# The last spectral mixing of a four-layer convolution kernel, as 32x32 products on the array's diagonal tiles

## What is computed

```
def _L3_conv_ref(x, weights):
    x_f = jnp.fft.rfft2(x)
    k_f = jnp.fft.rfft2(weights)
    out_f = jnp.einsum('bchw,ochw->bohw', x_f, k_f)
    return jnp.fft.irfft2(out_f, s=(H, W))
```

## Time and profile before

| What | us |
|---|---|
| median of 3 runs | 1059.65 |
| lowest, highest | 1059.22, 1061.24 |
| the profiled execution's own time | 1059.79 |
| its span in the trace | 1058.0 |
| PE busy | 894.0 |
| DVE busy | 661.6 |
| ACT busy | 520.3 |

### The profile page before, as it was taken

How to read it: one execution, slowest core, us unless ns; L and a number is a source line. 1 busy time by engine, 2 the same in 40 slices (tenths; PEclk the granted TensorE clock), 3 DMA queues, 4 the chain that set the end, 5 groups by cost and what they waited for, 6 DMA issues and landing times. The chain is left out here.

```text
span 1058.0 us, 25662 instructions
## 1 busy us (share of the span) xinstructions
PE 894.0 (85%) x9335; PEld 742.2 (70%) x9335; DVE 661.6 (63%) x1208; ACT 520.3 (49%) x900; POOL 122.2 (12%) x120
## 2 busy tenths in 40 slices
PE   6999999776468956488699999995888799998998
PEld 6999999765367953376544444443887699998998
DVE  3556464674585769689776665655666698871232
ACT  2444444575434437166379996001887423325554
POOL 0000000001001006156302222000000100001110
PEclk9999999898658989699899999997999899999999
DMA  6465757463300000000000000002200337740222
GB/s 251 160 241 192 271 212 220 119 155 81 93 4 1 0 14 1 0 1 0 0 1 1 0 0 0 0 0 52 44 0 0 80 81 159 145 94 1 95 105 117
DMA packets 47673, 79.12 MB, mean 75 GB/s; under 512 B 19322, under 2 KB 37888, under 8 KB 44816
## 3 DMA queue, kind: packets, MB, share of 16 engines
q1 hardware_dynamic: 30992, 61.80, 21.1%
q10 hardware_dynamic: 16640, 16.78, 4.6%
HBM read 50.65 MB, written 27.92 MB: 74 GB/s over the span
## 5 line engine op out<-in xcount | busy, mean ns | idle before, releaser
L1440 DVE SCALAR_TENSOR_TENSOR X<-bank,c_power,X 32x512 f32 x128 | 95.8, 748 | 60.4 <-PE bank L1408 55.4
L1565 PE MATMUL bank<-m_xp,m_kf 128*32 128x64 f32 x2048 | 116.8, 224 | 6.5 <-DVE m_xp L1533 5.1
L1565 PEld LDWEIGHTS bank<-m_xp,m_kf 128*32 128x32 f32 x2048 | 116.4, 139 | 6.9 <-issue 6.9
L1408 PE MATMUL bank<-c_rh,c_w_high 128*128 x288 | 111.0, 386 | 2.0 <-DVE c_rl L1353 2.0
L1408 PE MATMUL bank<-c_rh,c_w_low 128*128 x288 | 110.9, 385 | 0.0
L1408 PE MATMUL bank<-c_rl,c_w_high 128*128 x288 | 110.8, 385 | 0.0
L924 DVE TENSOR_TENSOR X<-X,bank 128x512 f32 x64 | 43.6, 681 | 91.2 <-PE bank L910 91.2
L205 DVE BATCH_NORM_STATS2 bn<-X 128x6 f32 x128 | 85.5, 683 | 2.4 <-POOL X L1212 1.6
L1581 ACT COPY xm<-bank 64x512 f32 x64 | 32.5, 585 | 95.3 <-PE bank L1565 95.3
L1367 ACT ACTIVATE c_r<-X,c_nrm 32x1024 f32 (+1 forms) x56 | 73.4, 1311 | 2.4 <-DVE c_nrm L1416 1.1
L439 DVE COPY ks_cols<-bank 128x512 f32<-128x512 f32 x64 | 42.6, 681 | 46.0 <-PE bank L405 46.0
(11 more groups left out here) (187 smaller groups left out, 1931.2 us busy)
## 6 DMA issues: line engine op xcount, KB each, us to landing
ks_src<-in_L_conv_weights SPq DMA_DIRECT2D x32, 512.0 KB, 6.3
kf<-ks_spec ACTq DMA_DIRECT2D x16, 1024.0 KB, 10.1
m_kf<-kf SPq DMA_DIRECT2D x32, 512.0 KB, 8.0
X<-in_x SPq DMA_DIRECT2D x4, 2048.0 KB, 12.9
out_y<-X SPq DMA_DIRECT2D x16, 512.0 KB, 2.7
xf<-f_xm SPq DMA_DIRECT2D x6, 448.0 KB
l_wb<-in_L_conv_weights_r SPq DMA_DIRECT2D x4, 512.0 KB, 13.0
l_wb<-in_L_conv_weights_i SPq DMA_DIRECT2D x4, 512.0 KB, 14.7
```

The costliest lines, as they stand in the source:

```text
L1408: m = pe.matmul(ps[n][:], w[:, ky, kx].rearrange("p o c -> p (o c)"), d[:, q, b, y:y + HALF, x:x + HN], start=i == 0, stop=i == len(terms) ...
L1440: dve.scalar_tensor_tensor(x, ps[n][o * C:(o + 1) * C, :].rearrange("p (y x) -> p y x", x=HN), filt.power[at, 2:3], x, ALU.mult, ALU.add). ...
L1565: last = pe.matmul(ps[4 * half + m // 8][at:at + C, m % 8 * N:(m % 8 + 1) * N], kf[p][:, j, :, H * half + m], xp[half][:, j, m].rearrange( ...
```

## The change

The last mixing takes xm as it lies. For each set, DVE writes a buffer xt with two parts: the spectra as they are, and the spectra multiplied by i (imaginary part negated, real part behind it). PE multiplies part 0 with the real part of the kernel's spectra and part 1 with the imaginary part, and adds the two in PSUM. Each product has 32x32 weights and 32x32 data, on one quarter g of the partitions, and writes the same quarter of the output; the four quarters follow one another, each at another frequency k so that they write to four different banks. That is 8 x 64 x 2 x 4 = 4096 products; the loop's body holds 1024 of them and is run four times. POOL's zeros are gone. ACT copies a whole set of 128 partitions out of PSUM. The kernel's spectra are loaded by one transfer of 2 MB for each set, in the layout in which kf lies in DRAM. In the first stage the stores of kf move from ACT's stream to SP's.

```diff
@@ kernel_spectra_stage, SP's stream
-                with sp.Fori(0, tiles // 2) as i:
-                    for p in range(2):
-
-                        sp.wait_ge(turned, START + 32 * i + 16 * p - 16)
-                        for k in range(4):
...
+                def store(i, p):
+                    sp.wait_ge(made_read, START + 32 * i + 16 * p + 16)
+                    for part in range(2):
+                        sp.dma_start(pr.kf[:, :, part, 2 * i + p, :].rearrange("s p n -> p s n"),
+                                     spec[:, :, part].rearrange("p s o k -> p s (o k)")).then_inc(stored, 16)
+
+                for p in range(2):
+                    load(0, p)
+                load_x(0)
+                with sp.Fori(1, tiles // 2) as i:
+                    for p in range(2):
+                        load(i, p)
+                        store(i - 1, p)
+                    load_x(i)
+                for p in range(2):
+                    store(tiles // 2 - 1, p)
                 filt.load(sp)
@@ kernel_spectra_stage, ACT's stream
-                        act.wait_ge(made_read, START + base + 16)
-                        for part in range(2):
-                            act.dma_start(pr.kf[:, :, part, 2 * i + p, :].rearrange("s p n -> p s n"),
-                                          spec[:, :, part].rearrange("p s o k -> p s (o k)")).then_inc(stored, 16)
@@ load_kernel_spectra
+    sp.dma_start(to[:].rearrange("p r o k -> p (r o k)"), pr.kf[s].rearrange("p r t n -> p (r t n)")
+                 ).then_inc(loaded, 16)
@@ l3_mix_stage, DVE's stream
+            def turn(dve, s, p):
+
+                dve.tensor_copy(xt[p][:, 0], xm[:, s])
+                dve.tensor_scalar(xt[p][:, 1, :, 0], xm[:, s, :, 1], -1.0, None, ALU.mult)
+                return dve.tensor_copy(xt[p][:, 1, :, 1], xm[:, s, :, 0])
...
@@ l3_mix_stage, PE's stream
+                with pe.Fori(0, SETS // 2) as i:
                     for p in range(2):
...
+                        for t in range(N):
+                            for part in range(2):
+                                for g in range(4):
+
+                                    k = (t + SPAN * g) % N
+                                    at = slice(g * C, (g + 1) * C)
+                                    last = pe.matmul(ps[4 * p + k // SPAN][at, k % SPAN * 2 * B:(k % SPAN + 1) * 2 * B],
+                                                     kf[p][at, part, :, k], xt[p][at, part, k].rearrange("p r b -> p (r b)"),
+                                                     start=part == 0, stop=part == 1)
+                        last.then_inc(mixed, 1)
@@ l3_mix_stage, ACT's stream
+                        act.wait_ge(mixed, START + 2 * i + p + 1)
+                        for n in range(4):
+                            c = act.copy(xm[:, 2 * i + p, SPAN * n:SPAN * n + SPAN].rearrange("p k r b -> p (k r b)"),
+                                         ps[4 * p + n][:])
+                        c.then_inc(mixed_read, 1)
```

More of the change, by code:

```diff
@@ L1455, in _ @@
             def _(sp):
-                load_kernel_spectra(sp, pr, kf0, 0, 0, loaded0)
+                load_kernel_spectra(sp, pr, kf0, 0, loaded0)
             @block.tensor
@@ L1502, in _ @@
             def _(sp):
-                load_kernel_spectra(sp, pr, kf[1], 0, 1, loaded[1])
-                with sp.Fori(1, PAIRS) as i:
+                load_kernel_spectra(sp, pr, kf[1], 1, loaded[1])
+                with sp.Fori(1, SETS // 2) as i:
                     for p in range(2):
[L1507 to L1520, removed]
+                        sp.wait_ge(mixed, START + 2 * i + p - 1)
+                        load_kernel_spectra(sp, pr, kf[p], 2 * i + p, loaded[p])
@@ L1535, in _ @@
[L1535 to L1538, removed]
-                    for p in range(2):
-                        for half in range(2):
-                            dve.wait_ge(mixed, START + 4 * i + 2 * p + half - 1)
-                            stage(dve, i, p, half).then_inc(staged, 2)
-            @block.gpsimd
-            def _(pool):
-                pool.memset(xp[0][0:2 * C, :, :, 1], 0.0).then_inc(zeroed, 1)
-                pool.memset(xp[0][2 * C:P, :, :, 0], 0.0).then_inc(zeroed, 1)
+                for p in range(2):
+                    last = turn(dve, p, p)
+                    if p == 0:
+                        packed = slice(0, N, N // 2)
+                        last.then_inc(fix, 1)
+                        dve.wait_ge(fix, 1)
+                        dve.memset(xt[0][0:C, 0, packed, 1], 0.0)
+                        dve.memset(xt[0][0:C, 1, packed, 0], 0.0)
+                        last = dve.tensor_copy(xt[0][0:C, 1, packed, 1], xm[0:C, 0, packed, 1])
+                    last.then_inc(turned, 1)
@@ L1549, in _ @@
+                with dve.Fori(1, SETS // 2) as i:
+                    for p in range(2):
+                        dve.wait_ge(mixed, START + 2 * i + p - 1)
+                        turn(dve, 2 * i + p, p).then_inc(turned, 1)
             @block.tensor
@@ L1552, in _ @@
                 pr.keep_warm(pe, 16)
[L1553 to L1554 removed]
+                with pe.Fori(0, SETS // 2) as i:
                     for p in range(2):
[L1556 to L1569 removed]
+                        pe.wait_ge(loaded[p], 16 * i + 16)
+                        pe.wait_ge(turned, 2 * i + p + 1)
+                        pe.wait_ge(mixed_read, START + 2 * i + p - 1)
+                        pe.sem_inc(pr.pace, 1)
+                        for t in range(N):
[7 more added lines that the diff above has]
+                        last.then_inc(mixed, 1)
             @block.scalar
@@ L1573, in _ @@
                 act.sem_inc(mixed_read, START)
[L1574 removed]
+                with act.Fori(0, SETS // 2) as i:
                     for p in range(2):
[L1576 to L1583 removed]
+                        act.wait_ge(mixed, START + 2 * i + p + 1)
[3 more added lines that the diff above has]
+                        c.then_inc(mixed_read, 1)
 def matrices(pr, ctx, shapes, dt=F32):
```

59 lines of the change are left out of this document (11 added, 48 removed).

## The result

| | before | after |
|---|---|---|
| median of the device time | 1059.43 us (4 runs) | 1224.71 us (4 runs) |
| ratio after / before | | 1.1548 [1.153, 1.1565] |
| span of the profiled execution | 1058.0 us | 1223.0 us |
| last mixing, first to last start of a record on PE | 118.5 us | 273.2 us |
| first product of the input transform (L237) | 200.97 us | 212.12 us |

A forecast was written before the change was run, and what follows sets the result against it. PE was taken as the bound, with fetching of code setting the new mixing's time: +130 mixing, -3 earlier start, +0.3 last copies, +15 first stage, +142 on 1059.8, 1202 us; 8-in-10 range 1125 to 1255.

The forecast's parts named there:

- The blocks: Last mixing on PE: 4 passes of 16 blocks of 256 instructions, each fetched anew in 3.73 us, 239 us.
- one and a half blocks already there: Start of the last mixing: the first code is already fetched, which saves only its stops, about -1 us.
- The jumps: Last mixing's loop: each of three jumps back costs one more block, 11 us together; ends none to 3 x 7.5.
- Queueing behind the loads of kf: Last mixing: a fetch may queue during 2 MB loads, 0 to 1.3 us each third block, up to 29 us.
- The clock does not enter: Last mixing: even at 1.2 GHz a block's 128 records take 2.42 us, less than the 3.73 of fetching.
- The first stage: End of the first stage: small loads now stand behind a store, delaying the next stage +15 us, ends +5 and +22.
- The earlier start: Last mixing: DVE's first staging takes 3.4 us, so PE starts earlier, -3 us.
- hidden staging, copies and loads of 2 MB: Last mixing: DVE's 3 us, ACT's 2.3 us and the loads of a set stay hidden under 31 us of PE.
- Rival 1: Last mixing: the loop body stays after its first pass; stage 118 to 176 us, total 1071 to 1129; chance 0.13.
- Rival 2: Last mixing: blocks fetched ahead, four quarters overlapping at full clock, 9.4 ns a record, 77 us; total 1030; chance 0.06.
- The stops: First layer's mixing: PE stops 1.0 to 1.6 us after each 128 records, read as waiting for the next code block.
- The 25 ns floor: Skill's claim that matmuls start no less than about 25 ns apart: stage 205 us, total about 1158; given no chance.

The follow-up runs named there:

- e2: Changed kernel with the four loop passes of the last mixing written out on PE, so no jump back: 1198.04 us, ratio 1.1319.
- e5: Changed kernel without the six 2 MB loads of kf inside the last mixing: 1203.97 us, ratio 1.1387.
- e1: Changed kernel with PE's mixing loop body cut to 4 blocks, the first 16 t multiplied four times, still 8192 records: 1088.87 us, ratio 1.0284.
- e8: First stage of the changed kernel with the last mixing of the kernel before: 1070.10 us, ratio 1.0113.
- e4: Changed kernel with all t from 32 on left out, so a body of 8 blocks and 4096 records: 1105.45 us.
- e6: e1 with 16 data columns in each product instead of 32: stage 135.4 us.
- e12: e1 with 64 data columns in each product instead of 32: stage 140.1 us.

## Why the prediction was right

**The blocks (239 us of the sum).** Right in kind and size. 67 large distances, 70 packets in the mixing (26 to 92 in all, "60 or more" was asked for), mostly 3.5 to 3.8 us from start to start. The -1 us for one and a half blocks already there did not come: PE stopped for 4.20 us after its first 127 records. e2, which has no jumps, took 248.5 us for 64 blocks; by the prediction 239.

**The jumps (11 us): the term that was mis-sized.** Three times one more block of 3.73 was assumed; e2 puts them at 24.7 us, 8.2 each, just past the end of 3 x 7.5 that the sum named as the highest. A third of it is contention: without loads of kf a pause is 6.8 us in place of 9.8, from start to start.

**Queueing behind the loads of kf (0 in the sum, up to 29 in the range).** No row stood behind the 1.3 us that the prediction gave each third block. Queueing cost 18.6 us by e5: 8.9 of it at the jumps (29.4 - 20.5), which are counted there, and 9.7 at the blocks. 249 + 13.7 for the jumps + 9.7 is 272.4, against 273.2 measured. These two terms are the 23 us by which the total was missed; the others come to about -1 us together, -4 of them in the first stage.

**The clock does not enter.** Right for the records: the clock was 0.50 behind the first 127 of them, and a turn of four took 57 ns there as in e1 at the full clock. The reason is stronger than the one given: the turn of 57 ns is the same at either level with up to 32 columns. Whether the stops follow the clock is not shown; every body of eight or more blocks ran at 0.50.

**The first stage (+15).** 11.15 at L237, e8 +10.6 by the medians: inside the ends of 5 and 22. c_raw took 7.34 us to issue and not 16.17, so the small packets suffered less than was taken. **The earlier start (-3)** was -3.7, and hidden staging, copies and loads of 2 MB cost nothing that shows.

**Rival 1** (the body stays) fell with the first pause at 913; e4 shows that half as long a body isn't kept either. **Rival 2** had two conditions. The overlap of quarters is real, and e1 gives it its price: 15.5 ns a record with all that is around it, where 13.0 was the point from which it decides. So even without stops behind the first pass the change would have lost: 1.0284 with e1, of which the first stage is 1.0113 by e8. The prediction didn't say so: it took 9.4 ns from halving 18.9 with the clock. That was its weakest step, since nothing in the rows showed that these records follow the clock, and they don't. So the direction would have come out right even if the account of fetching had been wrong; the size would not. (The 18.9 has the last record's some 240 ns in it; the starts are 17.1 ns apart, because some turns have two records.) **The stops** that speak against the rule "mostly hidden" (Trainium skill, Runtime: NRT & Kernel Launch, section Instruction fetch mechanics) are there 67 times over. The same section's 128 KiB, eight blocks, agrees with e4 as far as it goes: four blocks stayed, eight didn't. **The 25 ns floor** (TensorE: Matmul & The Clock Gate, section Wait — 56ns, not 53.3ns? in the Trainium skill) is again not what these traces show, where records start 14.4 ns apart on average on four tiles; its neighbour in that section, about 56 ns for 128 columns at the full clock, fits the records of 16-bit numbers in the kernel before (56 ns, L499 to L501 with 128 columns), while those of 32-bit numbers take 109, so its likeness to the 57 ns explains nothing. A page that the prediction left out bears on it more: the Trainium skill (TensorEngine Tiling (Array Packing), section Performance Considerations) says that a matmul has a fixed cost of about 60 cycles, so that very few columns take as long as 60, and advises not to take a tiling factor from a dimension that is already small. In kind that is what e6 and e12 show, 16 to 64 columns at one price, and it speaks against this change, which halves 64 columns. In size it is not: 60 cycles of 2.4 GHz are 25 ns (an estimate from the page's figure), and the turn here is 57. The same section has 64 rows give a factor of 2 by themselves; line 1163 agrees, with two records in 112 ns where one of 128 rows takes 109.

**What stays open.** What the turn of 57 ns consists of; why six blocks stay every second time; and the version that the last reading suggests, the products of the kernel before (128 rows, 64 columns, 2048 records) in an order that goes round the four output quarters. At four records in 58 ns PE would need 2048 x 14.5 = 30 us in place of 116.8, and the staging on DVE, 74.75 us busy in 99.3, and the loads would bound the stage: an estimate, it was not tried, and no stream read here has tiles of 128 rows that take turns. No kernel that was run and does the whole work beats the kernel before by more than can be measured.

## What to carry to other kernels

Count a PE stream in blocks of 256 instructions before you cut products smaller: code that isn't at hand costs 3.5 to 3.8 us a block here, though its 128 records take only 2, a loop body of four blocks is run from what was fetched, eight are not, and each jump back to a lost body costs 8 us more. Count records, not columns: up to 64 columns a record of 32-bit numbers costs its tile the same 57 ns at the full clock, and what hides it is that the next records go to other tiles. So look first at the order in which products go round the tiles, then at their shape; that this order alone gains was not tried. Records of 16-bit numbers are cheaper: in the kernel before those of 64 columns start 29 ns apart (L499 to L501). A store put in front of small loads in one queue delays all of them by the time until its data is ready, 11 us here; what the next stage needs goes in front.

## What the runs showed of the hardware that was not expected

- At the lower clock and at the full one a turn of four records takes the same 57 ns for 16 and 32 columns (e6 at 0.50, e1 at both levels). At 64 columns it doesn't: 107 ns in e12's stretches at 1.2 GHz (842.1 to 845.5, 848.9 to 855.7 and 872.8 to 879.6), 57 to 58 in the others.
- Kernels with as many records in the same time were granted different clocks: e6 ran its mixing at 0.50, e12 at 0.95 on average and e1 at 0.90, going back and forth between the levels. The stage's length doesn't show it but in e12's slow stretches; what decided the level is not shown.
- The pause at a jump back is longer than two stops of a block (9.6 against 1.7), and 3 us of it come and go with a transfer of 2 MB under way. Under such transfers a single packet of instructions took up to 2.07 us (at 883.2 in the changed kernel), without them at most 1.35 in the mixing (e5).
